# Second gating factor on GpSimd, and mixers split around the next FFN, in a fused scan, FFN, mixer and MoE kernel

## Chip, cores and metric

One core of one Trainium2 chip. The metric is the device time of one execution in microseconds; the kernel before took 1871.28 us (median of 3 runs, 1856.59 to 1882.85).

## What is computed

Four residual layers on x of 2048 tokens by 512, each on a layer norm of its input, all float32:

```python
# 1 selective scan
delta = softplus(x_dbl[:, :64] @ W_dt.T + b_dt); B, C = the next 16 + 16 columns of x @ W_xproj.T
h = exp(delta * A) * h + delta * x * B_t;  y_t = (h * C_t).sum(16 states);  out = y + x * D
# 2 FFN, 2048 inner columns
x = fwht(x * SU_ug) / 64
x = silu(x @ W_gate.T * ws_g) * (x @ W_up.T * ws_u)
out = (fwht(x * SU_dp) / 64) @ W_down.T * ws_dp
# 3 mixer, 1024 inner columns
x, z = split(x @ W_in.T);  x = x @ conv_w.T
out = (x * D * silu(z)) @ W_out.T
# 4 MoE: 64 experts, top 8, capacity 128, 192 inner columns
out = sum of w * (silu(x @ wg) * (x @ wu)) @ wd over the chosen experts
```

## The kernel before

Tokens go in four chunks of 512 (`NCH`, `CH`). Hadamard transforms and the mixer's convolution are folded into the weights on the chip (chunks 0 and 1), which are stored as high and low float32r parts, and read back through a ring of six buffers, one "quantum" at a time.

**The scan** is the spine. Chunk c has 16 states n. In each, DVE multiplies `bx` = u * B (L1062; B broadcast by PE, L557), scans four 128x512 tiles (L1071) whose decays ACT makes (L781, two buffers), and multiplies `hc` = bx * C (L1088); GpSimd adds `hc` to `y` (L1215). `hc` and `bx` have one buffer each.

**FFN and mixer** of earlier chunks are laid around the scan. A quantum is one weight block for 128 inner columns: "gate", "up" or "down", each 12 matmuls (high by high, high by low, low by high). A gate and an up block make a pair (tile) in two PSUM banks; then ACT makes tanh into `th` (L700), DVE multiplies th = (th + 1) * gate (L933) and th = up * cs * th (L937), ACT rounds the high part into `act8` (L705), GpSimd subtracts for the low part (L1221). `th` has two buffers. A "half" is eight pairs and then their eight down blocks, which sum in the four banks `PF` that the pairs used; DVE adds these to `xall` (L948, `down_added`). An FFN has two halves, a mixer one.

**The order** is written out by places: each state n of chunk c has four (`state_at(c, n, 0..3)`), the drain one for each quantum. `spread` deals quanta out to places evenly; every engine has a function `side(pos)` that does its share of a place, PE at `pos`, ACT's tanh and DVE's factors and adding one place later, high and low part two places later. Engines work in program order, so a place's work stands behind everything that is written ahead of it: on GpSimd the places of state n stand ahead of its y adding, on DVE place 3 stands behind `hc`. In chunk c the mixer of chunk c - 2 (24 quanta) has the places from (0, 2) to (5, 0), the FFN of chunk c - 1 (48 quanta) those from (5, 0) to (14, 1). Layer norm: statistics on DVE (`mixer_stats`, L911), the power on GpSimd, the scaled rows on ACT (L801), transposes on PE into two borrowed banks (L468), high part on ACT (L743), low part on DVE (L925). `xn2T` holds the FFN's operand, `xT` the mixer's.

**The drain** does the mixer of chunk 2, the FFN of chunk 3 and, after a stop for its norm, the mixer of chunk 3 (24 quanta), with routing between: for each of 16 token tiles the normed row (L1106), its transposes, logits (L657), the top 8, the places (L664) and eight scatters on GpSimd (L1295) into `slots`. A tile is started every five places. Then the experts run (L1391 to L1511).

PE's waits in `quantum`: gate j waits for the first factor of pair j - 2 (`S_hg`), up j for its second factor (`S_gt`), down 0 for the second factor of the last two pairs, every down j for its low part (`S_al`).

## Time and profile before

| what | value |
|---|---|
| profiled execution | 1878.37 us, span 1876.5 us |
| mean granted TensorE clock | 0.913 |
| busy: PE, DVE, ACT, POOL | 1535.4, 1059.2, 589.7, 791.7 us |
| first state of chunks 0, 1, 2, 3 begins | 48.4, 304.5, 574.3, 843.4 us |
| last `hc`'s adding begins | 1085.9 us |
| last down block of the last mixer ends | about 1402 us |
| experts begin | about 1479 us |

PE is the tensor engine, DVE the vector engine, ACT the scalar engine, POOL is GpSimd. Busy shares are means over stages with different bounds, so the stages are to be read one by one: which engine has no idle time there, and what the others wait for. Granted clock is TensorE's, as a share of 2.4 GHz; its other level is 0.5. Durations of instructions are in ns in the groups, in us in time lines.

### The profile page before, as it was taken

What the parts mean: (1) busy time and instruction counts of PE and PEld (TensorE: products, weight loads), DVE (VectorE), ACT (ScalarE), POOL (GpSimd) and SP (SyncE); (2) the same over time, 40 slices, a digit from 0 to 9 for tenths busy, and PEclk for the clock granted to TensorE, in tenths of its full rate; (3) what the DMA queues carried; (4) which work ended last, traced back from release to release, by engine and by line L of the source; (5) the groups of instructions that cost most, each with busy time, mean ns of one, the idle gap of its engine ahead of it and who ended that gap; (6) DMA issues with size and microseconds to landing.
All of it is one profiled execution on the core that took longest, in us unless ns stands there. A gap on an engine that the chain in (4) does not pass through costs nothing. (4 is left out here: it accounts for less than half of the span.)

```text
span 1876.5 us, 19337 instructions
## 1 busy us (share of the span) xinstructions
PE 1535.4 (82%) x5792; PEld 1045.6 (56%) x5792; DVE 1059.2 (56%) x1576; ACT 589.7 (31%) x1031; POOL 791.7 (42%) x491
## 2 busy tenths in 40 slices
PE   6899855698976998958999789999892399889883
PEld 2344322376755776747788667777671255445441
DVE  3787657876678876788788854545323122222220
ACT  3433522254433343533333331212210122222220
POOL 3356732355643444444354424757314332222222
PEclk9999977799987998979999889999895699999997
DMA  6676552168763775774566448986440599999997
GB/s 188 180 212 197 140 170 87 45 202 288 262 207 106 211 230 166 223 237 135 169 194 187 146 118 255 325 298 194 131 143 1 175 321 324 297 294 310 295 298 146
DMA packets 193536, 380.35 MB, mean 203 GB/s; under 512 B 20994, under 2 KB 95106, under 8 KB 192944
## 3 DMA queue, kind: packets, MB, share of 16 engines
q1 hardware_dynamic: 173424, 339.44, 58.8%
q0 software_dynamic: 20032, 39.92, 8.9%
q8 instruction: 40, 0.66, 0.1%
q14 instruction: 40, 0.33, 0.1%
HBM read 301.65 MB, written 124.35 MB: 227 GB/s over the span
## 5 line engine op out<-in xcount | busy, mean ns | idle before, releaser
L1215 POOL TENSOR_TENSOR y<-y,hc 128x2048 f32<-128x2048 f32 x64 | 293.0, 4578 | 320.5 <-DVE hc L1088 320.3
L1071 DVE TENSOR_TENSOR_SCAN bx<-bank,state,bx 128x512 f32<-128x512 f32 x256 | 312.1, 1266 | 4.7 <-ACT bank L781 3.4
L781 ACT ACTIVATE bank<-dl,an 128x512 f32<-128x512 f32 x256 | 170.5, 683 | 281.0 <-DVE bx L1071 280.9
L498 PE MATMUL bank<-xn2T,ring 128*128 128x512 f32 x576 | 232.7, 404 | 15.2 <-DVE xall L948 8.9
L499 PE MATMUL bank<-xn2T,ring 128*128 128x512 f32 x576 | 227.9, 396 | 0.0
L500 PE MATMUL bank<-xn2T,ring 128*128 128x512 f32 x576 | 227.7, 395 | 0.0
L1221 POOL TENSOR_TENSOR act<-th,act 128x512 fp32r<-128x512 f32 x96 | 123.9, 1292 | 240.9 <-ACT act L705 240.6
L1088 DVE TENSOR_TENSOR hc<-bx,bank 128x2048 f32<-128x2048 f32 x64 | 146.2, 2284 | 60.4 <-PE bank L564 53.3
L1400 PE MATMUL bank<-wgu,xeT 128*128 128x384 f32 x512 | 177.6, 490 | 0.0
L509 PE MATMUL bank<-ring,act 128*128 128x512 f32 x384 | 156.1, 407 | 20.6 <-DVE th L937 20.6
L1062 DVE TENSOR_TENSOR bx<-u,bank 128x2048 f32<-128x2048 f32 x64 | 146.1, 2283 | 34.0 <-PE bank L557 28.8
L511 PE MATMUL bank<-ring,act 128*128 128x512 f32 x384 | 153.1, 399 | 0.0
L510 PE MATMUL bank<-ring,act 128*128 128x512 f32 x384 | 152.8, 398 | 0.0
L1295 POOL DMA_INDIRECT slots<-row,idx x128 | 125.9, 984 | 52.8 <-issue 39.6
L498 PEld LDWEIGHTS bank<-xn2T,ring 128*128 128x128 f32 x576 | 110.2, 191 | 43.4 <-issue 21.1
L500 PEld LDWEIGHTS bank<-xn2T,ring 128*128 128x128 f32 x576 | 110.3, 191 | 24.3
L499 PEld LDWEIGHTS bank<-xn2T,ring 128*128 128x128 f32 x576 | 110.6, 192 | 23.0 <-issue 0.5
L1400 PEld LDWEIGHTS bank<-wgu,xeT 128*128 128x128 f32 x512 | 93.3, 192 | 51.9 <-issue 1.8
L1418 PE MATMUL bank<-wde,hT 96*128 96x512 f32 x256 | 120.5, 592 | 0.6 <-issue 0.6
L527 PE MATMUL bank<-raw_u,had 128*128 128x512 f32 x256 | 113.7, 594 | 0.4 <-DMA raw_u<-wgT_in 0.4
L1506 POOL DMA_INDIRECT out<-ye,tok x32 | 49.3, 1542 | 151.8 <-ACT ye L1455 138.3
L1480 DVE SCALAR_TENSOR_TENSOR te<-te,bank 128x192 f32<-128x192 f32 x64 | 22.7, 354 | 159.2 <-ACT te L1447 159.2
(150 smaller groups left out, 2379.5 us busy)
## 6 DMA issues: line engine op xcount, KB each, us to landing
ring<-w_all SPq DMA_DIRECT2D x288, 512.0 KB
wgu<-wgu_in SPq DMA_DIRECT2D x64, 768.0 KB
wde<-wd_in SPq DMA_DIRECT2D x64, 384.0 KB
slots<-empty_in SPq DMA_DIRECT2D x16, 1154.0 KB, 9.0
xe<-slots SPq DMA_DIRECT2D x64, 288.5 KB
w_all<-staged_u SPq DMA_DIRECT2D x64, 256.0 KB, 2.8
w_all<-fst SPq DMA_DIRECT2D x48, 256.0 KB, 3.2
w_all<-staged_d SPq DMA_DIRECT2D x32, 256.0 KB, 3.2
```

The lines of the kernel that those rows point to most:

```text
L498: nc.tensor.matmul(b[:, :], w[:, k, 0, :], x[:, 0, k, :], start=(k == 0), stop=False)
L499: nc.tensor.matmul(b[:, :], w[:, k, 0, :], x[:, 1, k, :], start=False, stop=False)
L500: last = nc.tensor.matmul(b[:, :], w[:, k, 1, :], x[:, 0, k, :], start=False, stop=(k == KT - 1))
L509: nc.tensor.matmul(PF[t][:, :], act8[:, 0, j, tok], w[:, 0, :], start=(j == 0), stop=False)
L510: nc.tensor.matmul(PF[t][:, :], act8[:, 0, j, tok], w[:, 1, :], start=False, stop=False)
L511: last = nc.tensor.matmul(PF[t][:, :], act8[:, 1, j, tok], w[:, 0, :], start=False, stop=(j == HALF - 1))
L781: nc.scalar.activation(dA[k % 2][:, :], dl[c % 2][:, k, :], ACT.Exp, scale=an[:, k, n:n + 1]).then_inc(S_dA, 1)
L1062: nc.vector.tensor_tensor(bx[:, :, :], u[:, :, :], PB[:, :].unsqueeze(1).to_broadcast([P, KT, CH]), ALU.mult).then_inc(S_bm, 1)
L1071: nc.vector.tensor_tensor_scan(bx[:, k, :], dA[k % 2][:, :], bx[:, k, :], state[:, k, n:n + 1], ALU.mult, ALU.add).then_inc(S_sc, 1)
L1088: nc.vector.tensor_tensor(hc[:, :, :], bx[:, :, :], PC[:, :].unsqueeze(1).to_broadcast([P, KT, CH]), ALU.mult).then_inc(S_cm, 1)
L1215: nc.gpsimd.tensor_tensor(y[c % 2][:, :, :], y[c % 2][:, :, :], hc[:, :, :], ALU.add).then_inc(S_ya, 1)
L1400: last = nc.tensor.matmul(CG[i % 2][:, 0:2 * FE], xeT[:, i % 2, k, :], wgu[:, i, k, :], start=(k == 0), stop=(k == KT - 1))
```

## The change

1. The second factor leaves DVE. ACT evicts the up bank, scaled by `cs`, into a new `ups` (two buffers, `up_out`), and GpSimd multiplies th = th * ups (`gated`). PE's up j waits for `ups` of pair j - 2; down 0 waits for the first factor and `ups` of the last two pairs.
2. The first factor (`half_gated`) is done one place after the gate block, not one after the up block.
3. Mixers of chunks 0 to 2 are two halves of four pairs and four down blocks. In chunk c the first part of mixer c - 2 (12 quanta) has the places from (0, 3) to (5, 0), the FFN those from (5, 0) to (13, 2), the second part (12 quanta) those from (13, 2) to (16, 1).
4. In the drain the second part of mixer 2 lies between FFN 3 and mixer 3, whose norm is made meanwhile. Eight tiles are routed beside the first 60 places, four (chunk 2) beside mixer 3, four behind it, as before.
5. Chunks' operands take turns in `tokT[c % 2]`; normed rows use `spr` (four tiles) in place of `xnt` (two).
6. Statistics for the mixer's norm move from (14, 1) to (13, 3).

```diff
-HALVES = [(kind, c, part) for c in range(NCH) for kind, part in (("ffn", 0), ("ffn", 1), ("mixer", 0))]
+FFN = [[("ffn", c, part, HALF * part, HALF) for part in range(2)] for c in range(NCH)]
+MIX = [[("mixer", c, part, 4 * part, 4) for part in range(2)] for c in range(NCH - 1)] + [[("mixer", NCH - 1, 0, 0, M1)]]
+HALVES = FFN[0] + [h for c in range(2, NCH + 1) for h in MIX[c - 2][:1] + FFN[c - 1] + MIX[c - 2][1:]] + MIX[NCH - 1]
...
-                first = PER * half_of["ffn", c - 1, 0]
                 if c >= 2:
-                    spread(quanta[first - PER:first], range(state_at(c, 0, 2), state_at(c, 5, 0)))
-                spread(quanta[first:first + 2 * PER], range(state_at(c, 5, 0), state_at(c, 14, 1)))
-            spread(quanta[-4 * PER:-PER], range(DRAIN + 2, DRAIN + 2 + 3 * PER))
-            spread(quanta[-PER:], range(DRAIN + 6 + 3 * PER, DRAIN + 6 + 4 * PER))
-            END = DRAIN + 6 + 4 * PER
+                    spread([("mixer", c - 2, 0)], range(state_at(c, 0, 3), state_at(c, 5, 0)))
+                spread([("ffn", c - 1, 0), ("ffn", c - 1, 1)], range(state_at(c, 5, 0), state_at(c, 13, 2)))
+                if c >= 2:
+                    spread([("mixer", c - 2, 1)], range(state_at(c, 13, 2), state_at(c + 1, 0, 1)))
+            START = DRAIN + 2
+            TURN = START + 5 * 12
+            END = TURN + 3 * 12
+            spread([("mixer", 2, 0), ("ffn", 3, 0), ("ffn", 3, 1)], range(START, TURN))
+            spread([("mixer", 2, 1), ("mixer", 3, 0)], range(TURN, END))
...
-            route_at = [DRAIN + 12 + 5 * i for i in range(12)] + [END + 1 + 3 * i for i in range(4)]
+            EARLY = 2 * TT
+            route_at = [DRAIN + 12 + 5 * i for i in range(EARLY)] + [TURN + 14 + 5 * i for i in range(TT)] + [END + 1 + 3 * i for i in range(TT)]
...
                             elif j >= 2:
-                                pe.wait_ge(S_gt, i - 1)
+                                pe.wait_ge(S_uc, i - 1)
...
                             if j == 0 and t % 2 == 0:
-                                pe.wait_ge(S_gt, HALF * h + HALF - 1 + t // 2)
+                                pe.wait_ge(S_hg, first_pair[h] + pairs - 1 + t // 2)
+                                pe.wait_ge(S_uc, first_pair[h] + pairs - 1 + t // 2)
...
+                    def up_out(h, j):
+                        i, m = first_pair[h] + j, tile_of(h, j)
+                        act.wait_ge(S_up, i + 1)
+                        wait(act, S_gt, i - 1)
+                        nc.scalar.activation(ups[:, i % 2, :], PF[2 * (j % 2) + 1][:, :], ACT.Copy, scale=cs[:, m:m + 1]).then_inc(S_uc, 1)
...
-                    def gated(h, j):
...
-                        dve.wait_ge(S_up, i + 1)
-                        dve.wait_ge(S_hg, i + 1)
-                        nc.vector.scalar_tensor_tensor(out=th[:, i % 2, :], in0=up[:, :], scalar=cs[:, m:m + 1],
-                                                       in1=th[:, i % 2, :], op0=ALU.mult, op1=ALU.mult).then_inc(S_gt, 1)
...
-                            if kind == "up":
-                                gated(h, j)
+                            if kind == "gate":
+                                half_gated(h, j)
...
+                    def gated(h, j):
+                        i = first_pair[h] + j
+                        pool.wait_ge(S_uc, i + 1)
+                        pool.wait_ge(S_hg, i + 1)
+                        nc.gpsimd.tensor_tensor(th[:, i % 2, :], th[:, i % 2, :], ups[:, i % 2, :], ALU.mult).then_inc(S_gt, 1)
...
+                        for h, kind, j in quanta_at.get(pos - 1, ()):
+                            if kind == "up":
+                                gated(h, j)
```

The order on DVE in chunk 3, states 13 and 14 (from one `bx` on), before; th rows are the factors, n_st, n_mvt and n_ngt the statistics:

```order
L1062 TENSOR_TENSOR bx<-u,bank 128x2048
L1071 SCALAR_TENSOR_TENSOR bx<-bank,state,bx 128x512 x4
L1088 TENSOR_TENSOR hc<-bx,bank 128x2048
L1062 TENSOR_TENSOR bx<-u,bank 128x2048
L1071 SCALAR_TENSOR_TENSOR bx<-bank,state,bx 128x512 x2
L948 TENSOR_TENSOR xall<-xall,bank 128x512 x4
L911 BN_STATS n_st<-xall 128x6 x4
L917 BN_AGGR n_mvt<-n_st 128x2 x4
L920 TENSOR_SCALAR n_ngt<-n_mvt 128x4
L1071 SCALAR_TENSOR_TENSOR bx<-bank,state,bx 128x512 x2
L1088 TENSOR_TENSOR hc<-bx,bank 128x2048
```

And on DVE in the same two states now:

```order
L1071 TENSOR_TENSOR bx<-u,bank 128x2048
L1080 SCALAR_TENSOR_TENSOR bx<-bank,state,bx 128x512 x4
L957 TENSOR_TENSOR xall<-xall,bank 128x512 x4
L1097 TENSOR_TENSOR hc<-bx,bank 128x2048
L946 SCALAR_TENSOR_TENSOR th<-th,bank 128x512
L925 BN_STATS n_st<-xall 128x6 x4
L931 BN_AGGR n_mvt<-n_st 128x2 x4
L934 TENSOR_SCALAR n_ngt<-n_mvt 128x4
L1071 TENSOR_TENSOR bx<-u,bank 128x2048
L1080 SCALAR_TENSOR_TENSOR bx<-bank,state,bx 128x512 x2
L946 SCALAR_TENSOR_TENSOR th<-th,bank 128x512
L1080 SCALAR_TENSOR_TENSOR bx<-bank,state,bx 128x512 x2
```

Adding and statistics moved from state 14 into state 13, and the first factors of the mixer's second part stand in both states.

The order on POOL in the drain, one routed tile beside the gate and up blocks of the FFN, before (act is the low part, slots the scatters):

```order
L1318 TENSOR_TENSOR n_vet<-n_mvt,eps 128x1
L1320 TENSOR_TENSOR n_rst<-n_vet,neghalf 128x1
L1295 DMA slots<-row,idx 8192x577 x2
L1221 TENSOR_TENSOR act<-th,act 128x512
L1295 DMA slots<-row,idx 8192x577 x4
L1221 TENSOR_TENSOR act<-th,act 128x512
L1295 DMA slots<-row,idx 8192x577 x2
```

And on POOL at such a tile now:

```order
L1336 TENSOR_TENSOR n_vet<-n_mvt,eps 128x1
L1338 TENSOR_TENSOR n_rst<-n_vet,neghalf 128x1
L1230 TENSOR_TENSOR th<-th,ups 128x512
L1313 DMA slots<-row,idx 8192x577 x2
L1236 TENSOR_TENSOR act<-th,act 128x512
L1313 DMA slots<-row,idx 8192x577 x2
L1230 TENSOR_TENSOR th<-th,ups 128x512
L1313 DMA slots<-row,idx 8192x577 x2
L1236 TENSOR_TENSOR act<-th,act 128x512
L1313 DMA slots<-row,idx 8192x577 x2
```

A product of `th` and `ups` stands between the scatters for each low part.

## Rows read from the trace of the kernel before

**Rows 1.** Groups of instructions: count, busy us and mean ns, idle before and releasers.

```profile
L1071 DVE TENSOR_TENSOR_SCAN bx<-bank,state,bx 128x512 f32<-128x512 f32 x256 | 312.1, 1266 | 4.7 <-ACT bank L781 3.4
L1215 POOL TENSOR_TENSOR y<-y,hc 128x2048 f32<-128x2048 f32 x64 | 293.0, 4578 | 320.5 <-DVE hc L1088 320.3
...
L1088 DVE TENSOR_TENSOR hc<-bx,bank 128x2048 f32<-128x2048 f32 x64 | 146.2, 2284 | 60.4 <-PE bank L564 53.3 <-POOL y L1215 5.7
L1062 DVE TENSOR_TENSOR bx<-u,bank 128x2048 f32<-128x2048 f32 x64 | 146.1, 2283 | 34.0 <-PE bank L557 28.8 <-DVE hc L1088 5.0
L1295 POOL DMA_INDIRECT slots<-row,idx x128 | 125.9, 984 | 52.8 <-issue 39.6 <-DVE idx L1148 12.3 <-ACT act L705 0.9
L1221 POOL TENSOR_TENSOR act<-th,act 128x512 fp32r<-128x512 f32 x96 | 123.9, 1292 | 240.9 <-ACT act L705 240.6
...
L937 DVE SCALAR_TENSOR_TENSOR th<-bank,cs,th 128x512 f32<-128x512 f32 x96 | 72.1, 751 | 38.9 <-PE bank L500 28.1 <-issue 2.9 <-DVE th L933 0.4
...
L700 ACT ACTIVATE th<-bank,gsh 128x512 f32<-128x512 f32 x96 | 65.4, 682 | 130.2 <-PE bank L500 104.0 <-POOL act L1221 16.0 <-issue 5.2
L933 DVE SCALAR_TENSOR_TENSOR th<-th,bank 128x512 f32<-128x512 f32 x96 | 64.9, 676 | 63.6 <-ACT th L700 61.8 <-issue 1.8
...
L705 ACT ACTIVATE act<-th 128x512 fp32r<-128x512 f32 x96 | 60.0, 627 | 112.7 <-DVE th L937 104.6 <-issue 7.4
...
L911 DVE BATCH_NORM_STATS2 n_st<-xall 128x6 f32<-128x512 f32 x64 | 41.8, 685 | 6.1 <-DMA xall<-x_in 5.4
...
L948 DVE TENSOR_TENSOR xall<-xall,bank 128x512 f32<-128x512 f32 x48 | 31.6, 685 | 29.0 <-PE bank L511 25.0 <-issue 2.5 <-remote 1.5
...
L712 ACT ACTIVATE staged_u<-bank,vec 128x512 fp32r<-128x512 f32 x32 | 21.1, 677 | 15.1 <-PE bank L527 15.0
```

**Rows 2.** Busy time in five stretches: length, PE, PEld, DVE, ACT, POOL, clock, DMA.

```profile
574.30:657.90 83.60, 75.15 (x330) 60.80 (x331) 71.47 (x74) 30.45 (x54) 36.00 (x20) 0.92 0.62 181
...
811.60:843.40 31.80, 12.46 (x50) 8.96 (x49) 27.95 (x29) 11.80 (x20) 7.24 (x6) 0.68 0.85 249
843.40:925.50 82.10, 74.06 (x325) 60.15 (x326) 66.98 (x65) 29.43 (x52) 34.63 (x17) 0.92 0.47 140
925.50:1056.70 131.20, 130.74 (x574) 107.33 (x573) 110.03 (x95) 44.62 (x77) 66.18 (x26) 1.00 0.65 193
1056.70:1085.90 29.20, 11.65 (x47) 8.48 (x45) 25.83 (x27) 8.23 (x14) 6.41 (x5) 0.71 0.24 73
```

**Rows 3.** PE's waits at the turns, whole span: us, times, longest.

```profile
PE bank L509 <- DVE th L937: 20.6, 11, 4.3
...
PE bank L498 <- DVE xall L948: 8.9, 4, 3.4
```

**Rows 4.** PE's time line at two turns and ahead of the last mixer.

```profile
716.72 0.50 PE L509 MATMUL bank<-ring,act 128*128 128x512 f32 x1 [2.64 <-DVE th L937]
...
745.31 0.77 PE L498 MATMUL bank<-xn2T,ring 128*128 128x512 f32 x1 [3.44 <-DVE xall L948]
...
1322.84 0.39 PE L511 MATMUL bank<-ring,act 128*128 128x512 f32 x1
...
1334.79 0.76 PE L498 MATMUL bank<-xn2T,ring 128*128 128x512 f32 x1 [1.46 <-issue]
```

**Rows 5.** POOL's time line in the drain: two tiles' first steps, one scatter.

```profile
1123.73 0.19 POOL L1318 TENSOR_TENSOR n_vet<-n_mvt,eps 128x1 f32<-128x1 f32 x1 [4.30 <-DVE n_mvt L1203]
...
1185.29 0.97 POOL L1295 DMA_INDIRECT slots<-row,idx  x1 [0.30 <-issue]
...
1306.18 0.19 POOL L1318 TENSOR_TENSOR n_vet<-n_mvt,eps 128x1 f32<-128x1 f32 x1 [2.51 <-DVE n_mvt L1203]
```

**Rows 6.** DVE's time line in the drain: a row that waits for its buffer.

```profile
1191.69 0.69 DVE L1106 TENSOR_SCALAR row<-xall,n_mvt,n_rst 128x512 f32<-128x512 f32 x1 [3.00 <-DMA slots<-row,idx]
```

**Rows 7.** The instructions of L1062: shortest, median and longest in ns.

```profile
L1062 DVE TENSOR_TENSOR bx<-u,bank x64: 2274/2286/2290, 48.4 to 1073.7; 128x2048 f32<-128x2048 f32 x64
```

More of the change, by code:

```diff
@@ L274, in returned @@
                 return S_rel, KT * c + i + 1
+            x3_half = [half_of["mixer", c, 1 if c + 1 < NCH else 0] for c in range(NCH)]
             def used(q):
@@ L411, in refill @@
                             i = number_of_quantum[q] + RING
-                            if i == PER * half_of["mixer", 0, 0]:
+                            if i < len(quanta) and quanta[i] == (half_of["mixer", 0, 0], "gate", 0):
                                 for s in S_ms:
@@ L419, in x3_out @@
                         for h, kind, j in quanta_at.get(pos - 2, ()):
-                            if HALVES[h][0] == "mixer" and (kind, j) == ("down", HALF - 1):
-                                c = HALVES[h][1]
+                            of, c, part = HALVES[h][:3]
+                            if of == "mixer" and (of, c, part + 1) not in half_of and (kind, j) == ("down", pairs_of[h] - 1):
                                 sp.wait_ge(S_de, TT * (h + 1))
```

127 lines of the change are left out of this document (64 added, 63 removed).

## The prediction

> **What bounds the kernel now.** I read four views, in this order: the groups of instructions, the busy time by stage, PE's waits, and the time lines around the turns. The program has a scan stage (chunks 0 to 3 of 16 states each), a drain of matmuls and routing from 1085.9 to 1402 us, the last routing up to 1479 us, and the expert stage, which the change doesn't touch.
>
> One scan state costs DVE 2.28 + 4 x 1.27 + 2.28 = 9.63 us, and each FFN or mixer tile adds 0.68 (L933) and 0.75 (L937) [rows 1]. One weight block ("quantum") is 12 matmuls. In the window 925.5 to 1056.7 us, PE is busy 130.74 of 131.2 us with 574 matmuls, so a quantum is 12 x 0.228 = 2.73 us [rows 2]. That window is states 5 to 13 of chunk 3: here **PE is the bound**, and DVE, 110 us busy, waits. States 0 to 4 (574.3 and 843.4 us on) are double bound: PE is busy 75.2 and 74.1 of 83.6 and 82.1 us with 24 mixer quanta, DVE 71.5 and 67.0. States 14 and 15 (811.6 and 1056.7 us on) are DVE's: PE has only the last three FFN quanta, 3 x 2.73 = 8.2 us of its 12.5 and 11.7, then idles, and its granted clock falls to means of 0.68 and 0.71 [rows 2]. So PE stands idle at each chunk's end, while the next states have more PE work than they can hide.
>
> Inside the PE-bound windows PE has gaps where a half of a layer turns: from up to down it waits for DVE's second factor (20.6 us in 11 waits), from down to the next gate for DVE's adding (8.9 us in four) [rows 3]. The matmul after the second kind took 0.77 us instead of 0.39 (the half-speed level, 1.2 GHz), and after the first kind 0.50 [rows 4].
>
> **The gating, part by part.** It takes 96 x 0.751 = 72 us off DVE (64 of the 96 in the scan), adds 96 ScalarE evictions, for which L712, the same operation from PSUM with a scale, stands at 0.677 (65 us), and 96 GpSimd multiplies; its subtraction L1221 of the same shape stands at 1.29 (124 us) [rows 1]. ACT is busy 44.6 of 131.2 us in the densest window and POOL 66.2 [rows 2]; 16 pairs more there make about 55 and 87. Both fit.
>
> *Turns.* Down now waits for the first factor (already done one place earlier) and ScalarE's 0.68 us. The first two token tiles take 6 x 0.228 = 1.4 us, which covers that, so most of the 20.6 us goes. Two of the 11 waits stand in the mixers' states, where the gain is lost; I take -15. The last down block of the first FFN half moves from a place ahead of `hc` to one ahead of the scans' end, so the adding no longer stands behind a 2.28 us `hc`: -5 of 8.9. Five quanta behind such gaps took 4.2 to 4.9 us instead of 2.7 at the lower clock; -10 in all. One more turn per chunk gives back 2. Together **-28**, bounds -36 and 0 (ACT may stand behind GpSimd when PE needs it).
>
> *The longer chain.* Second product, high part and low part now cross ACT, POOL, ACT, POOL. Where an `up` falls into a state's last place, its product stands behind the y adding (4.58) and one L1221: 4.58 + 1.29 + 1.29 = 7.2 us after `hc`, and the next tanh 0.63 + 0.68 later, 8.5; DVE gets to the first factor after 2.28 + 2.5 + 0.7 = 5.5. That is 3.0 us of wait in such a state. In the FFN states PE needs 5.65 x 2.73 + 0.5 = 15.9 us and DVE only about 11.5 to 13, so it hides. In state 10 of chunk 1 POOL gets the y adding and 13 operations of 128x512 (three weight splits, four corrections, six for pairs), 4.6 + 13 x 1.29 = 21.3 us, over PE's 15.9. I take **+5** for both, bounds 0 and +40.
>
> **The new spread.** *States 0 to 4* of chunks 2 and 3 lose 12 of 24 quanta, so DVE bounds them. From 71.5 and 67.0 us go 8 x 0.751 = 6.0 and four L933 (2.7); chunk 3 gets four L948 of the mixer's second part (2.7). That leaves 62.8 and 61.0, with 10 us of waits (12 and 15 before): 72.8 and 71.0 against 83.6 and 82.1, **-22**, bounds -30 and -14.
>
> *States 5 to 13* now have to be done in 8.5 states instead of 9.25. Since PE bounds them, the 48 quanta take the same 131 us: nothing is gained, and 0.75 states of DVE work land outside.
>
> *After the last FFN quantum* DVE must still do: adding 0.7, `hc` 2.3, a first factor 0.7, four statistics and the rest 3.6 (they moved ahead of state 14), state 14 with two factors 11.0, state 15 with one factor and two splits 11.7, waits of 3: 33 us. Before, it was 29.2 - 8.2 = 21. That is +12 in chunk 3, the same in chunk 2 (2.3 more on both sides), +8 in chunk 1, where no mixer lies. **+32**, bounds +20 and +36. This is what the first view hides: the idle PE time at the chunk's end is filled, but PE then idles in states 0 to 4 of the next one.
>
> *Drain.* Before, PE stood from the last down of the FFN (1323) to 1334.8 us for the final mixer's normalization, and then started at half speed [rows 4]. The mixer part of chunk 2 now lies there: -14. One turn more +1. But where routing and gate/up blocks overlap, POOL gets per five places 8 x (0.97 + 0.30) = 10.2, 0.8 for the power, 2.5 x 2.57 = 6.4, sum 17.4, plus up to 1 of issue; the period was on the mean 16.5 (eleven of them from 1123.7 to 1306.2 us [rows 5]). PE already waits there for a `row`, which waits for the landing of the scatter issued last at 1185.29 and seen at 1191.69 [rows 5, 6]; a later POOL moves it one for one. 36 gate/up places, 7.2 periods, at 2.2: +16, bounds 0 and +25. The last routes meet a POOL that isn't empty: +2. Sum **+5**, bounds -13 and +25.
>
> **Sum.** -28 + 5 - 22 + 32 + 5 = -8. The profiled execution took 1878.4 us (span 1876.5), so 1870 by its own time. It stands 7.1 above the median of the runs shown, 1871.3; on that footing the forecast is **1863 us**. A measurement of this kernel tells about 2% (37 us) from no change.
>
> GpSimd gets 124 us more, next to a busy DVE. The shortest, middle and longest `bx` take 2274, 2286 and 2290 ns, though the 4.6 us y addings run beside many of them [rows 7]: no blocking is seen. The Trainium skill ("SBUF — State Buffer", section "SBUF: two separate sides") says that a GpSimd operation and a DVE operation with two SBUF inputs hold their shared ports exclusively, the other blocking fully. By that rule the new multiplies could stop DVE; in this kernel `bx`, `hc`, scans and gating each take one input from PSUM, so the rule gives nothing here either, except for the four `u` products. Where a DVE operation of another kernel has both inputs in SBUF, it would.
>
> **Rivals.**
> 1. *DVE was the real bound* and PE's continuous run an effect of it: then the 48 us taken from it in the scan count whole. For it: PE waits for DVE 20.6 and 8.9 us. Against: no gap in the window 925.5 to 1056.7. It gives -48 in the scan, -13 in the drain: 1871 - 61 = 1810.
> 2. *GpSimd's chain becomes the bound* (slower). Place: the tanh behind the high part on ACT, which waits for a product behind the y adding. Price: 3.0 us a state, over 26 states with pairs, 78 us at most. In the PE-bound states 4 us of slack hide it; it decides once that wait exceeds them, or where PE is no longer the bound, the ten mixer states. With half of it (39), the drain's upper end (+9 over my value) and the turns' gain lost by a third (+9): 1863 + 57 = 1920.
> 3. *Only the drain goes wrong*: scatters, products and landings in a row, at the upper end, and the tail with it: 1863 + 20 = 1883.
> 4. *The ports block after all*, for 64 products of 1.29 us: 1863 + 83 = 1946.
> 5. *The spread does nothing*: idle time only moves from the chunk's end to the next states, as I hold for the most part; with turns unchanged too, 1871 + 20 = 1891.
>
> **How the numbers follow.** Forecast 0.56 (its own range 1840 to 1888), rival 1 0.15, rival 2 0.13, rival 3 0.08, rival 4 0.02, rival 5 0.06. Faster by over 2% (under 1834) holds most of rival 1 and a little of the forecast, 0.15; slower (over 1909) most of rival 2, rival 4 and a little of 3 and 5, 0.15; within 0.70. The range 1830 to 1906 leaves out most of rivals 1 and 2.
>
> **What would show it.** PE without waits at up-to-down turns, or only short ones; states 0 to 4 of chunks 2 and 3 at 71 to 73 us with PE at half its share; states 5 to 13 unchanged but for turns; from the last FFN quantum to the next chunk 33 us instead of 21; no 11 us gap ahead of the final mixer; scatter periods of about 19 us. I am wrong if states 5 to 13 shrink by more than the turns, if `th` on DVE waits for a tanh longer than in the kernel before, or if PE's clock falls to half in states 0 to 4.

## The result, and the profile after

The changed kernel took 1893.28 us (median of 4 runs, 1885.76 to 1907.78) against 1876.09 for the kernel before on the same chip (4 runs): ratio 1.0131, 95% interval 1.0073 to 1.0189. That is under the 2% bound, but above 1 by its whole interval: the change costs some 1.3%, where 0.4% less than before was forecast. The profiled execution took 1886.29 us (span 1884.5, mean granted clock 0.916).

Single profiles need care here. Chunk 0 took between 251 and 261 us in the fourteen profiles of this study, and the expert stage between 383 and 403, though their work is the same in all of them. So I compare the touched stages: chunks 1 to 3 (first `bx` of one to first `bx` of the next) and the drain (end of the last `hc` to the experts' first transposed row). Before they took 269.8, 269.1, 242.5 and 393.8 us, together 1175.2; after 280.4, 268.1, 244.2 and 404.9, together 1197.6. That is **+22.4 us**, 1.2% of the whole, and agrees with the timed ratio. (The two profiled executions as wholes differ by only 7.9 us, because chunk 0 took 5.0 us less and the experts 8.9 us less in the second one.)

The groups of instructions of the changed kernel, with the same columns as [rows 1]:

```profile
L1224 POOL TENSOR_TENSOR y<-y,hc 128x2048 f32<-128x2048 f32 x64 | 292.2, 4566 | 282.0 <-DVE hc L1097 282.0
...
L1080 DVE TENSOR_TENSOR_SCAN bx<-bank,state,bx 128x512 f32<-128x512 f32 x256 | 312.3, 1267 | 1.2
...
L1230 POOL TENSOR_TENSOR th<-th,ups 128x512 f32<-128x512 f32 x96 | 123.9, 1291 | 177.6 <-ACT ups L712 166.2
...
L514 PE MATMUL bank<-ring,act 128*128 128x512 f32 x384 | 156.9, 409 | 22.5 <-ACT ups L712 16.1
L946 DVE SCALAR_TENSOR_TENSOR th<-th,bank 128x512 f32<-128x512 f32 x96 | 65.9, 687 | 196.6 <-ACT th L706 196.4
...
L1236 POOL TENSOR_TENSOR act<-th,act 128x512 fp32r<-128x512 f32 x96 | 123.8, 1289 | 94.8 <-ACT act L717 94.4
...
L1313 POOL DMA_INDIRECT slots<-row,idx x128 | 126.7, 990 | 51.6 <-issue 38.2
```

The prices of the operations were right: 1.291 us for each GpSimd product (1.29 taken), and the 72 us of L937 [rows 1] are gone from DVE. What is new stands behind the bar, in the idle times. The first factor on DVE (L946) waited 196.4 us for tanh, against 61.8 for L933 [rows 1]; the prediction had named exactly this as a sign that it is wrong.

The windows of the changed kernel, as [rows 2]: chunk 2 in states 0 to 4, 5 to 13, 14 and 15, then the same of chunk 3.

```profile
579.40:649.70 70.30, 48.31 (x193) 36.22 (x194) 64.09 (x62) 28.41 (x50) 35.59 (x20) 0.84 0.43 132
649.70:818.80 169.10, 160.11 (x662) 127.17 (x662) 106.76 (x94) 76.18 (x126) 101.09 (x52) 0.95 0.66 199
818.80:847.40 28.60, 25.79 (x105) 20.74 (x104) 24.11 (x19) 16.89 (x29) 14.81 (x12) 0.88 0.62 184
847.40:914.90 67.50, 53.28 (x215) 40.48 (x213) 61.22 (x57) 27.76 (x49) 35.69 (x18) 0.90 0.58 187
914.90:1064.40 149.50, 144.84 (x627) 118.93 (x628) 106.31 (x93) 56.49 (x95) 86.60 (x43) 0.99 0.59 177
1064.40:1091.60 27.20, 24.40 (x98) 19.57 (x97) 22.01 (x18) 13.88 (x24) 16.14 (x13) 0.87 0.49 145
```

States 0 to 4 of chunks 2 and 3 took 70.3 and 67.5 us (before 83.6 and 82.1): the gain is there, and larger than forecast. States 5 to 15 took 197.7 and 176.7 (before 185.4 and 160.4): it is paid back there. PE is busy 160.1 of 169.1 and 144.8 of 149.5 us, no longer 130.74 of 131.2. The count behind PE's busy time shows more work in this window (627 matmuls instead of 574 in chunk 3), since the mixer's second part has moved in.

PE's waits, longest first, whole span; columns as in [rows 3]:

```profile
PE bank L472 <- DVE row L1115: 50.8, 13, 11.0
...
PE bank L514 <- ACT ups L712: 16.1, 5, 3.9
...
PE bank L502 <- DVE th L946: 10.6, 5, 4.7
...
PE bank L502 <- DVE xall L957: 8.7, 4, 3.7
...
PE bank L514 <- DVE th L946: 5.3, 1, 5.3
...
PE bank L514 <- POOL act L1236: 1.2, 2, 0.8
```

At the first matmuls of gates and downs PE waited 16.1 + 10.6 + 8.7 + 5.3 + 1.2 = 41.9 us. Before it was 20.6 + 8.9 [rows 3] and 2.0 for a first factor, 31.5:

```profile
PE bank L498 <- DVE th L933: 2.0, 1, 2.0
```

The waits from up to down, 20.6 us before, are 16.1 + 5.3 + 1.2 = 22.6 now: they changed their name and stayed. Those of a gate for a first factor grew from 2.0 to 10.6. The routed tiles' periods are read from POOL's time line, as [rows 5]:

```profile
1129.64 0.19 POOL L1336 TENSOR_TENSOR n_vet<-n_mvt,eps 128x1 f32<-128x1 f32 x1
...
1261.11 0.19 POOL L1336 TENSOR_TENSOR n_vet<-n_mvt,eps 128x1 f32<-128x1 f32 x1 [2.63 <-DVE n_mvt L1212]
```

These are the first and the eighth tile: seven periods of 18.8 us, against 16.4 in the same seven before. PE's wait for a routed row rose with them, from 34.4 to 50.8 us.

### The profile page after: what moved, and what is told of

Read it like the earlier page. It is cut to its first block and busy times, and to the rows that moved or that the text cites. A ratio compares the mean times of both kernels' runs of the same rounds, so it can differ in the third digit from the quotient of the medians.

```text
span 1884.5 us, 19575 instructions
## 1 busy us (share of the span) xinstructions
PE 1542.6 (82%) x5792; PEld 1049.3 (56%) x5792; DVE 1013.5 (54%) x1492; ACT 650.3 (35%) x1127; POOL 914.0 (49%) x587
## 5 line engine op out<-in xcount | busy, mean ns | idle before, releaser
L502 PE MATMUL bank<-tokT,ring 128*128 128x512 f32 x768 | 315.5, 411 | 22.9 <-DVE th L946 10.6
L503 PE MATMUL bank<-tokT,ring 128*128 128x512 f32 x768 | 308.4, 402 | 0.0
L504 PE MATMUL bank<-tokT,ring 128*128 128x512 f32 x768 | 308.1, 401 | 0.0
L1230 POOL TENSOR_TENSOR th<-th,ups 128x512 f32<-128x512 f32 x96 | 123.9, 1291 | 177.6 <-ACT ups L712 166.2
L502 PEld LDWEIGHTS bank<-tokT,ring 128*128 128x128 f32 x768 | 150.0, 195 | 61.7 <-issue 31.9
L514 PE MATMUL bank<-ring,act 128*128 128x512 f32 x384 | 156.9, 409 | 22.5 <-ACT ups L712 16.1
L946 DVE SCALAR_TENSOR_TENSOR th<-th,bank 128x512 f32<-128x512 f32 x96 | 65.9, 687 | 196.6 <-ACT th L706 196.4
L504 PEld LDWEIGHTS bank<-tokT,ring 128*128 128x128 f32 x768 | 149.6, 195 | 33.3
L503 PEld LDWEIGHTS bank<-tokT,ring 128*128 128x128 f32 x768 | 149.8, 195 | 30.8 <-issue 0.5
L1524 POOL DMA_INDIRECT out<-ye,tok x32 | 49.3, 1542 | 145.6 <-ACT ye L1473 131.2
```

What stands on the lines that cost most here:

```text
L502: nc.tensor.matmul(b[:, :], w[:, k, 0, :], x[:, 0, k, :], start=(k == 0), stop=False)
L503: nc.tensor.matmul(b[:, :], w[:, k, 0, :], x[:, 1, k, :], start=False, stop=False)
L504: last = nc.tensor.matmul(b[:, :], w[:, k, 1, :], x[:, 0, k, :], start=False, stop=(k == KT - 1))
L514: nc.tensor.matmul(PF[t][:, :], act8[:, 0, j, tok], w[:, 0, :], start=(j == 0), stop=False)
```

## The experiments

All times in us from the profiled execution; "touched" is the sum of the four stages before it, and the ratio is that of timed runs against the kernel before on the same chip, with its 95% interval. Only e2 differs from the kernel before by more than the 2% bound; what is said of the others rests on the intervals and on the stages.

| kernel | chunk 1 | chunk 2 | chunk 3 | drain | touched | ratio |
|---|---|---|---|---|---|---|
| before | 269.8 | 269.1 | 242.5 | 393.8 | 1175.2 | 1 |
| after | 280.4 | 268.1 | 244.2 | 404.9 | 1197.6 | 1.0131 (1.0073 to 1.0189) |
| e1_spread_only | 270.7 | 266.3 | 248.8 | 388.0 | 1173.8 | 1.0007 (0.9959 to 1.0055) |
| e2_gating_only | 276.7 | 273.4 | 242.4 | 416.2 | 1208.7 | 1.0276 (1.0206 to 1.0347) |
| e3_add_later | 285.2 | 261.0 | 244.2 | 402.9 | 1193.3 | 1.0144 (1.0065 to 1.0223) |
| e4_three_th | 280.6 | 267.5 | 243.4 | 408.8 | 1200.3 | 1.0131 (1.0063 to 1.0200) |
| e5_tanh_first | 278.0 | 264.1 | 241.9 | 404.7 | 1188.7 | 1.0133 (1.0047 to 1.0218) |
| e6_factor_at_up | 272.7 | 265.7 | 246.5 | 402.3 | 1187.2 | 1.0088 (1.0051 to 1.0125) |
| e7_pool_in_scan | 281.9 | 267.3 | 243.4 | 389.8 | 1182.4 | 1.0061 (1.0016 to 1.0107) |
| e8_six_two | 269.8 | 259.7 | 243.0 | 392.5 | 1165.0 | 0.9971 (0.9932 to 1.0010) |
| e9_drain_only | 268.8 | 269.2 | 242.4 | 387.1 | 1167.5 | 0.9957 (0.9923 to 0.9992) |
| e10_turn_inside | 269.8 | 265.1 | 239.0 | 384.7 | 1158.6 | 0.9865 (0.9807 to 0.9924) |
| e11_inside_pool_scan | 277.4 | 269.5 | 236.5 | 383.0 | 1166.4 | 0.9962 (0.9927 to 0.9998) |
| e12_pool_chunk3 | 269.8 | 263.4 | 236.9 | 384.5 | 1154.6 | 0.9900 (0.9860 to 0.9940) |

**The two halves of the change, apart.** e1 keeps the new places and the new drain, gives the second factor back to DVE, and puts the first back to the up block's place:

```diff
-                                pe.wait_ge(S_uc, i - 1)
+                                pe.wait_ge(S_gt, i - 1)
...
+                        dve.wait_ge(S_up, i + 1)
+                        dve.wait_ge(S_hg, i + 1)
+                        nc.vector.scalar_tensor_tensor(out=th[:, i % 2, :], in0=PF[2 * (j % 2) + 1][:, :], scalar=cs[:, tile_of(h, j):tile_of(h, j) + 1],
+                                                       in1=th[:, i % 2, :], op0=ALU.mult, op1=ALU.mult).then_inc(S_gt, 1)
...
-                            if kind == "gate":
+                            if kind == "up":
```

> The kernel after with the second factor back on DVE (L937's form, at the up block's place, PE waits for it as before); spread, split mixers and drain stay. Theory A (the chain over ACT and GpSimd costs): the loss goes; DVE's wait for tanh falls from 196 us to about 70, states 5 to 13 of chunk 1 fall from 180 to about 168 us, scatter periods beside gate and up blocks fall from about 19 to 16.5 us, the drain is some 15 us shorter than in the kernel after: 1860 us, ratio to before 0.985 to 0.995. Theory B (the new spread costs, the gating is free): as slow as the kernel after or slower, ratio 1.00 to 1.02, since DVE has 72 us more.

e2 is the kernel before with parts 1 and 2 of the change alone (`ups`, `up_out`, the product on GpSimd, the first factor at the gate's place):

```diff
+                        nc.gpsimd.tensor_tensor(th[:, i % 2, :], th[:, i % 2, :], ups[:, i % 2, :], ALU.mult).then_inc(S_gt, 1)
...
-                            if kind == "up":
-                                gated(h, j)
+                            if kind == "gate":
+                                half_gated(h, j)
```

> The kernel before with the new gating alone (ScalarE evicts the up product, GpSimd multiplies, first factor a place earlier); whole mixers at their old places, old drain. Theory A: slower than before by 10 to 25 us, ratio 1.005 to 1.015, DVE's wait for tanh near 190 us. Theory B: not slower, ratio 0.98 to 1.00, the mixer's states 0 to 4 of chunks 2 and 3 shorter by 4 us each, since 6 us of DVE work go there.

Measured: 1.0007 and 1.0276. In both the gating is what costs (theory A), but both ratios lie above the ranges of that theory: e1 only comes back to the kernel before, and e2 loses about twice what was expected. The new places and drain by themselves are worth nothing (chunks 1 to 3 +4.4, drain -5.8), and the gating by itself costs: +33.5 us in the touched stages in the old layout, +23.8 in the new one (after less e1). (The timed ratio of e2 says some 50 us, at least 38; its profiled execution, 1903.28 us, is its fastest run, so its stages may show the loss too small.) Of the +23.8 in the new layout, chunk 1 holds 9.7 and the drain 16.9; chunks 2 and 3 hold +1.8 and -4.6. So the loss sits in two places, and each got experiments of its own.

**What in the gating costs?** e3 moves each `y` adding on GpSimd behind the next state's first place, so that products no longer stand behind it there:

```diff
+                                if m == 0 and n:
+                                    add(c, n - 1)
...
-                            add(c, n)
+                        add(c, NS - 1)
```

> The kernel after with GpSimd's y adding of state n one place later, behind the low part and product of the next state's place 0. Theory A in the form that the y adding (4.6 us) ahead of the product holds the chain: DVE's wait for tanh falls from 196 us to under 150, the scan gets 8 to 20 us shorter, ratio 0.995 to 1.005. Theory B, or a chain that is long for other reasons (ACT behind DVE's scans): no change beyond 3 us, ratio 1.01.

e4 gives `th` and `ups` a third buffer, with the waits one pair looser:

```diff
-            ups = sb(A, "ups", [P, 2, CH])
+            ups = sb(A, "ups", [P, 3, CH])
...
-            th = sb(A, "th", [P, 2, CH])
+            th = sb(A, "th", [P, 3, CH])
...
-                        wait(act, S_al, i - 1)
+                        wait(act, S_al, i - 2)
```

> The kernel after with three buffers in place of two for th and for the scaled up product. If tanh waits because GpSimd's low part releases th late (12 us of ACT's waits, and what queues behind them), DVE's wait for tanh falls by 30 us or more and the scan by 5 to 15 us, ratio 1.00. If tanh is late because it stands behind the high part on ACT, nothing changes: ratio 1.01, wait near 190 us.

e5 lets ScalarE do a place's tanh and `ups` ahead of the high part of an earlier pair:

```diff
-                        for h, kind, j in quanta_at.get(pos - 2, ()):
-                            if kind == "up":
-                                gated_hi(h, j)
...
+                        for h, kind, j in quanta_at.get(pos - 2, ()):
+                            if kind == "up":
+                                gated_hi(h, j)
```

> The kernel after with ScalarE's order in a place turned round: tanh and the scaled up eviction first, then the high part, which waits for GpSimd's product. Theory A1 (tanh is late because it stands behind a high part that waits for GpSimd): DVE's wait for tanh falls from 196 us by 60 or more, drain and scan together 10 to 20 us shorter, ratio to before 1.00 to 1.005. Theory A2 (in the drain GpSimd has too much to do between scatters; in the scan the first factor simply waits for PE's gate block, which costs nothing): no change beyond 4 us, ratio 1.01 to 1.015.

Measured: 1.0144, 1.0131, 1.0133, none to be told from the changed kernel. In e3 chunk 2 gains 7.1 us, but chunk 1 gives back 4.8. Buffers are not it: DVE waited 195.3 us for tanh with three of them and 196.4 with two. In e3 it waited 194.8. e5 takes 2 to 4 us out of each chunk's profile, which the timed runs don't confirm, and the wait falls to 170.5 us, where theory A1 wanted 60 less. The wait of DVE for tanh is therefore not a shortage of buffers, not the y adding, and not mainly a matter of ScalarE's order within a place.

e6 puts the first factor back to the up block's place, and leaves the product on GpSimd:

```diff
-                            if kind == "gate":
+                            if kind == "up":
                                 half_gated(h, j)
```

> The kernel after with the first factor back at the up block's place, as in the kernel before; the second stays on GpSimd. If DVE's 196 us of waiting for tanh is only that it now arrives earlier, the wait falls to about 60 us and the time stays within 4 us, unless DVE's routing steps stand behind that wait, in which case the drain (405 us from the last y adding's start to the experts) gets 5 to 10 us shorter. If the early factor helped, the turns on PE get longer: 5 to 10 us slower in the scan.

Measured: 1.0088; chunk 1 falls from 280.4 to 272.7 us, within 2.0 of e1, and DVE's wait for tanh falls from 196.4 to 99.3. The expectation had no such gain in it: it looked for one in the drain (which gets 2.6 us shorter) or for a loss in the scan. The timed ratio alone doesn't settle it, as its interval overlaps that of the changed kernel; but all five kernels with the early factor and the FFN in 8.5 states took 278.0 to 285.2 us for chunk 1, and the two with the late factor 270.7 and 272.7. **In this layout the earlier first factor is what costs chunk 1 its 8 us.** Of the 7.7 us, 6.6 lie in state 6 (21.7 us against 15.1). The time line of its end in the changed kernel shows how (start, duration, instruction, in brackets the idle time before it and its releaser):

```profile
408.84 0.63 ACT L731 ACTIVATE fst<-praw 128x512 fp32r<-128x512 f32 x1 [3.41 <-DMA praw<-winzT_in]
...
409.38 0.61 ACT L717 ACTIVATE act<-th 128x512 fp32r<-128x512 f32 x1
...
409.90 0.67 ACT L706 ACTIVATE th<-bank,gsh 128x512 f32<-128x512 f32 x1
...
410.60 0.69 DVE L946 SCALAR_TENSOR_TENSOR th<-th,bank 128x512 f32<-128x512 f32 x1 [4.23 <-ACT th L706]
...
411.20 2.28 DVE L1071 TENSOR_TENSOR bx<-u,bank 128x2048 f32<-128x2048 f32 x1
```

ScalarE stands in its queue for a weight load (`praw`, one of 16 plain weight splits that lie in chunk 1). The tanh is behind it, the first factor behind the tanh, and in DVE's program order `bx` of the next state behind the factor. Three such waits for tanh in state 6 cost DVE 10.3 us. The load's wait is no news: it was 44.1 us on ScalarE before and 40.0 after. Before, DVE came to its factors one place later and mostly found them ready: in chunk 1 it waited 16.4 us (7 times) for tanh, now 52.3 (15 times).

This holds for the FFN in 8.5 states. With the FFN at its old places, chunk 1 loses as much with the early factor (e2, 6.9 us more than before) as with the late one (e11 below, 7.6 us more than e10). There the place of the first factor is worth nothing in chunk 1, and the loss comes from the longer chain itself.

**The drain.** e7 keeps the changed kernel in the scan, and from the mixer of chunk 2 on gives the second factor back to DVE and the first its old place:

```diff
+            late = half_of["mixer", 2, 0]
+            in_drain = lambda h: h >= late
...
-                                pe.wait_ge(S_uc, i - 1)
+                                pe.wait_ge(S_gt if in_drain(h) else S_uc, i - 1)
...
-                            if kind == "gate":
+                            if kind == ("up" if in_drain(h) else "gate"):
                                 half_gated(h, j)
...
-                            if kind == "up":
+                            if kind == "up" and not in_drain(h):
                                 gated(h, j)
```

> The kernel after with the new gating in the scan's 64 pairs only; the 32 pairs of the drain have the second factor on DVE, as in the first experiment. Theory A2 (GpSimd between scatters): the drain is as long as with all gating on DVE, 388 us against 405, the scan as in the kernel after, 1044 us: ratio 1.000 to 1.004. If the cost lay in the scan: no change of the drain beyond 5 us, ratio 1.01.

Measured: the drain takes 389.8 us instead of 404.9, the ratio falls to 1.0061. With the products off GpSimd the routed tiles follow each other every 17.5 us (seven periods, 1133.34 to 1256.14) instead of 18.8, and PE waits 38.0 us for their rows instead of 50.8. Of the 15.1 us some 2.6 belong to the first factor's place (404.9 in the changed kernel, 402.3 in e6), so the products themselves are left with about 12.5. One tile's row of work on GpSimd in the changed kernel:

```profile
1189.67 1.25 POOL L1230 TENSOR_TENSOR th<-th,ups 128x512 f32<-128x512 f32 x1
1191.09 1.04 POOL L1313 DMA_INDIRECT slots<-row,idx  x1 [0.17 <-issue]
1192.43 0.98 POOL L1313 DMA_INDIRECT slots<-row,idx  x1 [0.30 <-issue]
1193.43 1.30 POOL L1236 TENSOR_TENSOR act<-th,act 128x512 fp32r<-128x512 f32 x1
...
1197.18 1.32 POOL L1230 TENSOR_TENSOR th<-th,ups 128x512 f32<-128x512 f32 x1
```

GpSimd is filled from 1188.9 to 1204.7 us without a pause of more than 0.31 us: products and low parts stand between the scatters, and each puts the last scatter of the tile off by its 1.3 us.

**Which layout is worth something?** e8 is e1 with mixers 0 and 1 as six pairs and two, the FFN's places and the norm's statistics as before (not in the lines shown), and the two late pairs from (14, 1) over the chunk's end:

```diff
-MIX = [[("mixer", c, part, 4 * part, 4) for part in range(2)] for c in range(NCH - 1)] + [[("mixer", NCH - 1, 0, 0, M1)]]
+MIX = [[("mixer", c, 0, 0, 6), ("mixer", c, 1, 6, 2)] for c in range(2)] + [[("mixer", 2, 0, 0, 4), ("mixer", 2, 1, 4, 4)]] + [[("mixer", NCH - 1, 0, 0, M1)]]
...
-                spread([("ffn", c - 1, 0), ("ffn", c - 1, 1)], range(state_at(c, 5, 0), state_at(c, 13, 2)))
+                spread([("ffn", c - 1, 0), ("ffn", c - 1, 1)], range(state_at(c, 5, 0), state_at(c, 14, 1)))
...
-                    spread([("mixer", c - 2, 1)], range(state_at(c, 13, 2), state_at(c + 1, 0, 1)))
+                    spread([("mixer", c - 2, 1)], range(state_at(c, 14, 1), state_at(c + 1, 0, 1)))
```

> All gating on DVE, drain as in the kernel after, but the FFN back at its 37 places (5, 0) to (14, 1), and the mixers of chunks 0 and 1 split into six pairs in the states 0 to 4 and two pairs behind the FFN. If squeezing the FFN into 8.5 states costs what the split brings: chunks 2 and 3 take 72 + 154 + 35 and 70 + 132 + 32 us, 261 and 234 against 266 and 249 with the spread of the kernel after, and chunk 1 about 268: the scan 20 us shorter than in the first experiment, ratio to before 0.985 to 0.993. If PE's and DVE's waits depend on the turns and not on the squeeze: 0.997 to 1.003.

Measured: 0.9971. Chunk 2 came as expected (259.7), chunk 3 did not (243.0): its states 0 to 4 took 81.3 us, as before the change. PE's time line in state 0 of chunk 3 has the cause:

```profile
834.19 0.79 PE L512 MATMUL bank<-ring,act 128*128 128x512 f32 x1 [5.43 <-DVE th L940]
838.70 0.77 PE L512 MATMUL bank<-ring,act 128*128 128x512 f32 x1 [1.58 <-POOL act L1224]
```

The second part's turn from up to down fell on the chunk's end, where DVE has `hc`, `bx` and the norm's work ahead of the factor: 5.43 us, and the matmuls behind the two waits take 0.79 and 0.77 us instead of 0.39. e9 and e10 followed. e9 leaves the scan as before and takes the new drain alone (lines against e8):

```diff
-MIX = [[("mixer", c, 0, 0, 6), ("mixer", c, 1, 6, 2)] for c in range(2)]
+MIX = [[("mixer", c, 0, 0, 8)] for c in range(2)]
...
-                    spread([("mixer", c - 2, 0)], range(state_at(c, 0, 3), state_at(c, 5, 0)))
+                    spread([("mixer", c - 2, 0)], range(state_at(c, 0, 2), state_at(c, 5, 0)))
```

> The scan's places and the gating as in the kernel before (mixers of chunks 0 and 1 are one half of eight pairs at (0, 2) to (5, 0)); only the drain is laid out anew (second part of mixer 2 between FFN 3 and mixer 3, eight tiles routed beside the first 60 places). Theory A (the drain's layout is worth some 6 us by itself, as the spread alone showed with other states ahead of it): scan ends at 1034 to 1040 us, drain 385 to 391 us, ratio 0.996 to 0.998. Theory B (the drain's 6 us came from the state in which the other scan leaves PE and the ring): drain 393 to 395 us, ratio 1.000.

e10 is e8 with the second part's places ending inside state 15:

```diff
-                    spread([("mixer", c - 2, 1)], range(state_at(c, 14, 1), state_at(c + 1, 0, 1)))
+                    spread([("mixer", c - 2, 1)], range(state_at(c, 14, 1), state_at(c, 15, 3)))
```

> As e8, but the six quanta of the mixer's second part have the places (14, 1) to (15, 2), one each, so that the turn and the adding fall into state 15 of the same chunk and not into state 0 of the next. Theory A (in e8 states 0 to 4 of chunk 3 lost their gain, 81.3 instead of 71 us, to the turn that stood in state 0): states 0 to 4 of chunk 3 take 71 to 75 us and states 14 and 15 of chunks 2 and 3 take 31 to 36 us; ratio 0.990 to 0.995. Theory B (18 quanta are simply too many for the states, or the time reappears in 14 and 15): states 0 to 4 of chunk 3 79 to 82 us or 14 and 15 38 us; ratio 0.996 to 1.000.

Measured: e9 0.9957, drain 387.1, as theory A said: the drain's layout is worth 6.7 us by itself. e10 0.9865, better than either theory gave; states 0 to 4 of chunk 3 took 72.9 us, 14 and 15 took 34.9 in chunk 3 and 39.5 in chunk 2 (over the 36 expected, and what theory B said). Its windows, states 0 to 4, 5 to 13, 14 and 15 of chunk 3:

```profile
839.50:912.40 72.90, 59.30 (x249) 47.72 (x250) 64.20 (x62) 27.12 (x47) 29.66 (x15) 0.88 0.61 186
912.40:1043.60 131.20, 130.74 (x574) 107.35 (x573) 110.04 (x94) 44.63 (x77) 66.18 (x26) 1.00 0.62 185
1043.60:1078.50 34.90, 27.22 (x119) 21.14 (x118) 28.49 (x32) 10.66 (x18) 8.98 (x7) 1.00 0.52 149
```

The middle row is the window of [rows 2] again, to 0.02 us: the FFN is left where PE is saturated. The last row is the difference: the idle end of the chunk, at a mean clock of 0.71 before, now holds 27.2 us of PE's work at 1.00. The touched stages give 1158.6, 16.6 us or 0.9% less than before; the timed ratio says 1.35%, and its interval (0.6% wide to either side, six runs) holds both. Two comparisons keep this in measure. Against e8, chunks 2 and 3 together are no shorter (502.7 us in e8, 504.1 in e10): states 14 and 15 took what states 0 to 4 gave, and the gain lies in the drain (392.5 to 384.7), whose first gate block now starts 3.7 us after the last `hc` and not 10.9, with no down block left over ahead of it. Against e9, which has the new drain alone, the split of the mixers is worth 8.9 us of the 16.6.

**The new gating in the best layout.** e11 is e10 with the product on GpSimd in the scan, first factor at the up block's place, and both factors on DVE in the drain:

```diff
+                            elif kind == "up" and not in_drain(h):
+                                up_out(h, j)
...
+                            if kind == "up" and not in_drain(h):
+                                gated(h, j)
```

> e10 with the second factor of the scan's halves on GpSimd (products scaled out by ScalarE), the first factor left at the up block's place, and the drain's gating on DVE. Theory A (in the scan DVE's 48 us of second factors lie in states that PE bounds, or are paid back as waits for the longer chain, so the new gating is worth nothing there even at its best place): chunks 1 to 3 within 3 us of e10's 269.8, 265.1 and 239.0, ratio 0.985 to 0.990. Theory B (with the first factor back at its place the freed DVE time counts in the ten states 0 to 4 of chunks 2 and 3, which DVE bounds, 0.75 us for each of 12 pairs, and in 14 and 15): chunks 2 and 3 shorter by 4 to 9 us each, ratio 0.978 to 0.983. Theory C (the chain over ACT and GpSimd costs time by itself): chunks 1 to 3 longer by 3 to 8 us in all, ratio 0.989 to 0.993.

Measured: 0.9962; chunks 1 and 2 lose 7.6 and 4.4 us, chunk 3 gains 2.5. That is theory C for chunks 1 and 2, in sum 9.5 against the 3 to 8 expected, and A or B for chunk 3; the ratio lies above all three ranges. What sets chunk 3 apart, as far as I can see, is GpSimd's other work: chunk 1 has 16 weight splits (L1282) and four pairs of softplus corrections for the next chunk (L1289, L1291), chunk 2 the corrections, chunk 3 neither. The time line of e11 in chunk 2, states 11 and 12, GpSimd first, then who waits:

```profile
765.76 1.29 POOL L1249 TENSOR_TENSOR act<-th,act 128x512 fp32r<-128x512 f32 x1 [0.81 <-ACT act L723]
767.01 1.30 POOL L1289 TENSOR_TENSOR spc<-dl,spc 128x512 f32<-128x512 f32 x1
768.39 1.30 POOL L1291 TENSOR_TENSOR spr<-spr,spc 128x512 f32<-128x512 f32 x1
769.65 1.29 POOL L1289 TENSOR_TENSOR spc<-dl,spc 128x512 f32<-128x512 f32 x1
771.02 1.29 POOL L1291 TENSOR_TENSOR spr<-spr,spc 128x512 f32<-128x512 f32 x1
772.26 4.60 POOL L1237 TENSOR_TENSOR y<-y,hc 128x2048 f32<-128x2048 f32 x1
776.83 1.30 POOL L1243 TENSOR_TENSOR th<-th,ups 128x512 f32<-128x512 f32 x1
777.00 2.29 DVE L1110 TENSOR_TENSOR hc<-bx,bank 128x2048 f32<-128x2048 f32 x1 [4.77 <-POOL y L1237]
...
778.16 0.63 ACT L723 ACTIVATE act<-th 128x512 fp32r<-128x512 f32 x1 [8.09 <-POOL th L1243]
778.70 0.67 ACT L718 ACTIVATE ups<-bank,cs 128x512 f32<-128x512 f32 x1
...
779.51 0.47 PE L505 MATMUL bank<-tokT,ring 128*128 128x512 f32 x1 [1.33 <-ACT ups L718]
```

GpSimd has no gap from 767 to 778 us. Corrections and adding delay the product, ScalarE waits 8.09 us for it with the next eviction behind it in its queue, and PE waits for that eviction. DVE waits as well, 4.77 us for the adding, which has to free `hc`. States 11 and 12 took 19.7 and 19.2 us, against 15.0 and 16.6 in e10.

e12 is e11 with the product on GpSimd for the halves of chunk 3 alone. It tests in which chunks the product costs; no run takes the splits or corrections away, so that they are the reason is read from the time line and not shown.

```diff
+            early = half_of["mixer", 1, 0]
-            in_drain = lambda h: h >= late
+            in_drain = lambda h: h >= late or h < early
```

> e10, with the second factor on GpSimd (up product scaled out by ScalarE, first factor at the up block's place) for the halves laid in chunk 3 alone: both parts of mixer 1 and FFN 2. In chunk 3 GpSimd has no weight splits. Theory A (the new gating costs time where GpSimd also splits folded weights, in chunks 1 and 2, because its products and the y adding queue behind those splits): chunks 1 and 2 as in e10, 269.8 and 265.1 us within 2 us, chunk 3 at 235 to 239 us, ratio 0.985 to 0.990. Theory B (the chain over ScalarE and GpSimd costs turns everywhere): chunk 3 at 242 us or more, ratio 0.990 to 0.994.

Measured: chunk 1 269.8, chunk 2 263.4, chunk 3 236.9, ratio 0.9900. (What its expectation calls splits of folded weights are in chunk 2 the corrections just shown.) The loss in chunks 1 and 2 went with the products, and chunk 3 kept a gain of 2.1 us over e10 in the profile, which the timed runs are too coarse to confirm: the intervals of e10 and e12 overlap. Both beat both kernels by their whole intervals, though the kernel before by less than 2%. DVE was relieved in states 5 to 13 of chunk 3, and they took the same time as before (in [rows 2] DVE is busy 110.03 us):

```profile
908.20:1039.40 131.20, 130.37 (x572) 107.01 (x571) 98.83 (x79) 54.96 (x93) 86.34 (x42) 1.00 0.62 185
```

## Why the prediction was wrong

The forecast was -8, the touched stages gave +22.4. By its steps:

- **Turns, -28: this step failed.** The prediction said that ScalarE's 0.68 us would hide under the first two token tiles, so that most of the 20.6 us goes, and 5 of the 8.9 with it. The waits from up to down came to 22.6 us and those for the adding to 8.7. All PE's waits at gates and downs were 41.9 us instead of 31.5, and that rise is the layout's: e1, with the same layout and both factors on DVE, has 28.5 + 8.1 + 7.7 = 44.3.

```profile
PE bank L512 <- DVE th L940: 28.5, 9, 5.5
...
PE bank L501 <- DVE xall L951: 8.1, 4, 3.2
PE bank L501 <- DVE th L936: 7.7, 3, 4.8
```

  So the new gating took 2.4 us off these waits (1.4 if the 1.0 us for `ups` at up blocks is counted), where 28 us were to come from the turns, and in the old layout (e2, 44.0 with 8.3 at up blocks, against 31.5) it added 12.5. The prediction priced the eviction and not its place in ScalarE's program order. The longest such case in chunk 2 shows it:

```profile
784.99 0.69 ACT L795 ACTIVATE bank<-dl,an 128x512 f32<-128x512 f32 x1 [2.01 <-DVE bx L1080]
786.17 0.69 ACT L795 ACTIVATE bank<-dl,an 128x512 f32<-128x512 f32 x1 [0.48 <-DVE bx L1080]
786.80 0.67 ACT L712 ACTIVATE ups<-bank,cs 128x512 f32<-128x512 f32 x1
...
787.61 0.77 PE L514 MATMUL bank<-ring,act 128*128 128x512 f32 x1 [3.90 <-ACT ups L712]
```

  Two decays of the scan stand ahead of `ups`, and both wait for DVE's scans. PE was freed of DVE by name and still waited for it, one engine further on, and then restarted at 0.77 us a matmul. The 10 us for slow blocks weren't won either: the first matmul of a token tile in the down blocks took 407 ns on the mean before (L509) and 409 ns after (L514). The prediction's own bound for this step reached up to 0; I had written "ACT may stand behind GpSimd", and it was behind DVE and a DMA.
- **Longer chain, +5 (bounds 0 and +40): mis-sized in chunk 1.** Gating cost 9.7 us there. The cause that I named, GpSimd's 21.3 us in one state, is a part (e11 lost 7.6 us in chunk 1 with the first factor at its old place, in the layout of e10; in that of e6 it was 2.0). The larger part in the changed kernel is one that I had counted as a help, the first factor one place earlier: 7.7 us between after and e6 (in the old layout it makes no difference, e2 against e11).
- **States 0 to 4, -22: right in kind, low in size.** 72.8 and 71.0 forecast, 70.3 and 67.5 measured, together -27.9. The shares were not as reckoned: 12 of the 22 were to come from the second factors that leave DVE, but e1, which keeps them there, has 70.9 and 71.5, so the layout gave 23.4 of the 27.9 and the gating 4.6.
- **After the last FFN quantum, +32.** In sum over states 5 to 15 chunks 2 and 3 rose by 12.3 and 16.3 us, beside the 12 each that this step gave before any gain at turns. That is in line with the step, though the chunks share it otherwise than I had it: with the gating left out (e1) states 5 to 15 rose by 0.8 us in chunk 1, not 8, by 10.0 in chunk 2 and by 16.9 in chunk 3. Filling the end of a chunk is no loss by itself: e10 does it too, and its states 5 to 15 of chunk 3 took 166.0 us, 5.6 more than before. It leaves the FFN's places and the norm's statistics alone, fills with half as many quanta and keeps the turn inside the chunk; which of these counts most no run separates, but for the turn (e8 against e10).
- **Drain, +5 by -14, +1, +16, +2; measured +11.1.** The layout alone gave -5.8 (e1) and -6.7 (e9), where -13 was taken. In e9 the part up to the end of the last mixer's adding shrank by 10.2 us (316.9 to 306.7), as the gap of 11 us ahead of the last mixer went, but the tail behind it grew by 3.5, from 76.9 to 80.4. It grew in every kernel with the new drain, with products on GpSimd or not, and stayed at 76.9 in e2: so the +2 that I gave to a busier GpSimd belongs to the layout. The +16 for GpSimd among the scatters has the right size, 15.1 us between after and e7, and in part by luck. It was reckoned as 2.2 us in each of 7.2 periods. The period did rise from 16.4 to 18.8 us, but e1 and e9, without products, already have 17.3 and 17.7; from e7 to after it rises by 1.2, which is 8.8 us in seven periods. The rest stands behind the eighth tile, and 2.6 us of the 15.1 are the first factor's.
- **Rivals.** Rival 5 came nearest, by its time (1891 against 1893.28 measured) and by its two conditions: the spread is worth nothing (e1 1.0007) and the turns are unchanged. It had a chance of 0.06, and it doesn't hold the losses in chunk 1 and in the drain. Rival 2 had the direction and the engine chain, and its price of a half (39 us of 78) was far too high: after less e1 the gating cost 6.9 us in chunks 1 to 3, and in chunk 3 it gained. Rival 3 had the drain, at 6 us over the value forecast instead of 20. Rival 1 is refuted by e12 for the states in which it differs from the forecast: with DVE busy 98.8 us instead of 110.0, states 5 to 13 of chunk 3 took 131.2 us as before. Rival 4: `bx` took 2272, 2286 and 2290 ns (shortest, middle, longest) with 64 products more on GpSimd in the scan, the times of [rows 7]. By the Trainium skill's rule ("SBUF — State Buffer", section "SBUF: two separate sides") a VectorE operation contends with a GpSimd one that reads SBUF when it has two SBUF inputs, and with any GpSimd one when it runs in a two-port mode; `bx` has one input in SBUF, and its times agree with the rule. No operation with two was looked at.

By halves of the change the miss is plain. The terms of the gating (-15 and -10 at the turns, chain +5, -12 in states 0 to 4, drain +16 and +2) sum to -14, and after less e1 gave +23.8. The terms of the layout (-5 and +2 at the turns, the other -10 in states 0 to 4, +32, drain -14 and +1) sum to +6, and e1 less before gave -1.4. Without the turns' -28 the forecast would have been +20, which is rival 5, and +22.4 was measured; that these agree is partly luck, since the other misses nearly cancel: states 0 to 4 came out 6 us better, the drain 6 worse, chunk 1 some 5 worse. These sizes are differences of profiles, good to two or three us each.

## What to carry to other kernels

An operation moved off a loaded engine costs more than its duration on the new one: look at what stands ahead of it in that engine's program order, and for what that waits (here scans on DVE and a weight load), since the old dependence comes back through that queue. A factor done as early as it can be may be a wait put at the head of an in-order engine: here it cost 7.7 us in chunk 1 with the FFN packed into 8.5 states and nothing there with the FFN at its old places, so leave it at the place where its input is ready for certain unless a run shows a gain. When idle time at a stage's end is to be filled, fill it without touching the stretch in which the bound engine is saturated, and keep a dependent turn off the point where the other engines change over: six pairs and two, with the turn inside state 15, gave 0.9% by its stages and 1.35% timed, where four and four, with the same drain, gave nothing.
